# Attention: K padded per head by GpSimd, Q dense for four heads, batch loop written out

## What is computed

```python
def _L1_attn_ref(x, w_in, b_in, w_out, b_out):
    B, S, E, H = (2, 256, 128, 16)
    ...
    qkv = x @ w_in.T + b_in
    q, k, v = jnp.split(qkv, 3, axis=-1)
    ...
    scores = jnp.einsum('bhqd,bhkd->bhqk', q * scale, k)
    ...
    attn = jax.nn.softmax(scores, axis=-1)
    out = jnp.einsum('bhqk,bhkd->bhqd', attn, v)
```

## Time and profile before

| | |
|---|---|
| median of three runs | 2952.7 us |
| span of the profiled execution | 3037.0 us |
| attention phase in it | about 1973 to 2772 us |
| TensorE busy, matmuls, of the span | 84% |
| VectorE busy | 75% |
| ScalarE busy | 59% |
| GpSimd busy | 45% |

### The profile page before, as it was taken

One profiled execution on the slowest core, in us unless ns is written; L12 is line 12 of the kernel. 1 busy time (PEld: TensorE's weight loads), 2 busy tenths in 40 slices (PEclk: granted clock), 3 DMA queues, 4 the chain that ended last, 5 costly groups with the idle time before them and its releaser, 6 DMA issues. The chain is left out here.

```text
span 3037.0 us, 38397 instructions
## 1 busy us (share of the span) xinstructions
PE 2549.4 (84%) x11128; PEld 1669.2 (55%) x11128; DVE 2285.1 (75%) x3877; ACT 1790.3 (59%) x3099; POOL 1373.7 (45%) x1486
## 2 busy tenths in 40 slices
PE   6888477888888888868887689969988889887999
PEld 5766233343344344227676568746555556554887
DVE  6887478989999999998786544478777777774444
ACT  3566465657556656524666445547777667665555
POOL 2365488888988988961563630021121121111000
PEclk9999688999999999998998789979999999998999
DMA  2246222222222222221345200020000000001000
GB/s 69 55 130 123 79 68 67 75 69 72 70 74 74 77 73 74 77 71 39 75 130 96 73 21 1 0 95 1 1 1 1 2 1 1 1 1 39 7 8 14
DMA packets 99804, 152.38 MB, mean 50 GB/s; under 512 B 12940, under 2 KB 50572, under 8 KB 99028
## 3 DMA queue, kind: packets, MB, share of 16 engines
q1 hardware_dynamic: 82052, 98.41, 10.6%
q0 software_dynamic: 17040, 51.07, 6.8%
q10 hardware_dynamic: 512, 0.53, 0.1%
HBM read 131.08 MB, written 18.87 MB: 49 GB/s over the span
## 5 line engine op out<-in xcount | busy, mean ns | idle before, releaser
L1750 POOL TENSOR_TENSOR a_hc<-a_H,a_cb 128x512 f32<-128x512 f32 x512 | 620.0, 1233 | 134.3 <-DVE a_H L1614 127.3
L1406 PE MATMUL a_Y<-a_hc,ident 128*128 128x512 f32 x1024 | 535.3, 633 | 57.0 <-POOL a_hc L1750 48.6
L2216 DVE TENSOR_REDUCE a_mx<-a_W 128x1 f32<-128x512 f32 (+3 forms) x768 | 397.2, 550 | 153.3 <-PE a_W L2005 99.6
L2116 ACT ACTIVATE a_pt<-a_W 128x512 f32<-128x512 f32 (+3 forms) x768 | 353.5, 493 | 224.1 <-PE a_W L2018 220.7
L1532 ACT ACTIVATE a_dA<-a_dt,a_aneg 128x512 f32<-128x512 f32 x512 | 342.6, 714 | 193.8 <-POOL a_dt L1769 103.2
L1406 PEld LDWEIGHTS a_Y<-a_hc,ident 128*128 128x128 f32 x1024 | 183.0, 196 | 307.6 <-POOL a_hc L1750 212.7
L1638 DVE TENSOR_TENSOR a_BX<-a_u,a_BX 128x1024 f32<-128x1024 f32 x256 | 308.6, 1211 | 44.0 <-PE a_BX L1340 22.3
L1614 DVE TENSOR_TENSOR_SCAN a_H<-a_dA,a_H,a_BX 128x512 f32<-128x512 f32 x256 | 312.5, 1264 | 2.5 <-ACT a_dA L1532 2.5
L2018 PE MATMUL a_W<-a_Q,a_K 128*128 128x512 f32 (+3 forms) x768 | 302.3, 399 | 4.1 <-ACT a_pt L2116 2.0
L1614 DVE TENSOR_TENSOR_SCAN a_H<-a_dA,a_BX 128x512 f32<-128x512 f32 x256 | 296.7, 1202 | 1.1 <-POOL a_hc L1750 1.0
L2002 PE MATMUL a_W<-a_K,a_Q 128*128 128x512 f32 (+3 forms) x768 | 273.9, 363 | 20.4 <-DVE a_K L2283 9.9
(11 more groups left out here) (327 smaller groups left out, 5628.4 us busy)
## 6 DMA issues: line engine op xcount, KB each, us to landing
a_cb<-a_crow SPq DMA_DIRECT2D x256, 256.0 KB, 3.1
m_orows<-m_yt SPq DMA_DIRECT2D x46, 256.0 KB
a_Q<-attention_zeros POOLq DMA_DIRECT2D x3, 2048.0 KB, 13.3
t_wst<-ternary_w SPq DMA_DIRECT2D x22, 256.0 KB, 2.7
m_xrows<-m_pool SPq DMA_DIRECT2D x16, 256.0 KB, 2.3
m_xg<-m_xrows,m_gidx POOLq DMA_INDIRECT x184
out<-x SPq DMA_DIRECT2D x8, 256.0 KB, 2.3
m_wg<-moe_ws SPq DMA_DIRECT2D x2, 516.0 KB, 4.5
```

The lines of the kernel that those rows point to most:

```text
L1406: pe.matmul(Y[:, h, :], ident[:], hc[:, g % HCRING, :], start=False, stop=v == NS - 1).then_inc(s_y, 1)
L1750: pool.tensor_tensor(hc[:, G % HCRING, :], H[:, s, span], cb[:, v % RING, :], ALU.mult).then_inc(s_hc, 1)
L2116: act.activation(pt[:, u % PR, 0:BLK - r * P], W[:, 3 + u % 3, 0:BLK - r * P], ACT.Exp).then_inc(s_exp, 1)
L2216: dve.tensor_reduce(dst, W[:, s % 3, 0:min(BLK, (t + 1) * P - c * BLK)], AX, ALU.max)\
```

## The change

K is padded in place of Q. K now has a copy per head and Q one dense tile per group. VectorE's combination of K lands in `stk`; GpSimd multiplies `stk` by a column of `heads` (one on the head's 32 rows, zero elsewhere) into each head's copy (`keys`): 128x512, four per chunk, eight per slot. Q's combination lands in Q directly. ScalarE's copies are gone, as are the zeroing of Q and the three transfers; a small load of `heads` is new. K is projected first (uses 0 and 2), Q afterwards (4 and 5). The maxima are added to Q in one addition of 128 rows. In GpSimd's queue two multiplications stand behind the mask of step 2, two behind that of step 3, and four behind the split of the maxima that follows. In the pre slot sixteen stand ahead of the first split. The loop over sequences 1 and 2 is a Python loop, all waits are on constants.

```diff
-            uses.update({0: ("Q", rel, n, 0), 2: ("Q", rel, n, 1), 4: ("K", rel, n, 0), 5: ("K", rel, n, 1),
+            uses.update({0: ("K", rel, n, 0), 2: ("K", rel, n, 1), 4: ("Q", rel, n, 0), 5: ("Q", rel, n, 1),
                          6: ("V", rel, n // 2, n % 2)})
...
-        with eng.Fori(1, NBATCH - 1) as i:
+        for i in range(1, NBATCH - 1):
...
-        Q, K = sb("Q", [P, GROUPS * GH, SEQ], F32R), sb("K", [P, GROUPS, SEQ], F32R)
+        Q, K = sb("Q", [P, GROUPS, SEQ], F32R), sb("K", [P, GROUPS * GH, SEQ], F32R)
...
-        ZEROS = tuple((Q[:, n:n + GH, :].rearrange("p h c -> p (h c)"), w["zeros"].bitcast(F32R))
-                      for n in range(GH, GROUPS * GH, GH))
...
-                    pe.matmul(W[:, 3 + u % 3, 0:BLK - r * P], K[:, g, tile(kt)],
-                              Q[:, g * GH + j, c * BLK + r * P:(c + 1) * BLK],
+                    pe.matmul(W[:, 3 + u % 3, 0:BLK - r * P], K[:, g * GH + j, tile(kt)],
+                              Q[:, g, c * BLK + r * P:(c + 1) * BLK],
...
-                                    pe.wait_ge(s_q, 2 * G + 4)
+                                    pe.wait_ge(s_k, 2 * G + 4)
...
-                def queries(i, use, j):
...
-                    last = act.activation(Q[head(j), n * GH + j, chunk(c)], stk[head(j), c, :], ACT.Copy)
...
-                    if kind == "max" and j < 2:
-                        for jj in (2 * j, 2 * j + 1):
-                            q = Q[head(jj), n * GH + jj, chunk(c)]
-                            ins = dve.tensor_tensor(q, q.bitcast(F32), M[head(jj), :], ALU.add)
-                        if j == 1:
-                            last = ins
+                    if kind == "max" and j == 0:
+                        q = Q[:, n, chunk(c)]
+                        last = dve.tensor_tensor(q, q.bitcast(F32), M[:], ALU.add)
...
-                for dst, src in ZEROS:
-                    pool.dma_start(dst, src).then_inc(s_zero, 16)
                 pool.wait_ge(s_xn, 1)
-                pool.memset(Q[:, 0:GH, :].bitcast(F32), 0.0).then_inc(s_cst, 1)
...
+                def keys(G, n, c, js):
+
+                    if js[0] == 0:
+                        pool.wait_ge(s_ld, 16 * len(LOADS))
+                        pool.wait_ge(s_st, 4 * G + c + 1)
+                    for j in js:
+                        last = pool.tensor_scalar(K[:, n * GH + j, chunk(c)], stk[:, c, :].bitcast(F32),
+                                                  heads[:, j:j + 1], 1.0, ALU.mult, ALU.mult)
+                    if js[-1] == GH - 1:
+                        last.then_inc(s_k, 1)
+
                 def slot(stage, i, g):
                     G = i * GROUPS + g
+                    n = (g + 2) % GROUPS
+                    ahead = stage not in ("last", "tail") or (stage == "last" and g + 2 < GROUPS)
+                    if stage == "pre":
+                        keys(0, 0, 0, range(GH))
+                        keys(0, 0, 1, range(GH))
+                        keys(1, 1, 0, range(GH))
+                        keys(1, 1, 1, range(GH))
                     if has_exp(stage):
                         split_max(stage, i, g, G, g, 1)
                         for v in DIAG[:TPB]:
                             mask_step(i, g, v)
+                            if ahead and v >= 2:
+                                keys(G + 2, n, 0, range(2 * (v - 2), 2 * (v - 1)))
                     if has_max(stage, g):
                         split_max(stage, i, g, G + 1, (g + 1) % GROUPS, 0)
                     if has_exp(stage):
+                        if ahead:
+                            keys(G + 2, n, 1, range(GH))
                         for v in DIAG[TPB:]:
                             mask_step(i, g, v)
```

More of the change, by code:

```diff
@@ L1895, in has_max, with all_slots @@
         return stage != "tail" and not (stage == "last" and g + 1 == GROUPS)
-    def all_slots(slot, eng):
+    def all_slots(slot):
         slot("pre", 0, -1)
@@ L1920, in attention @@
         wo, bo = sb("wo", [P, P]), sb("bo", [P, P])
-        mask = sb("mask", [P, P])
+        mask, heads = sb("mask", [P, P]), sb("heads", [P, GH])
         idr, mneg = sb("idr", [P, P], F32R), sb("mneg", [P, P], F32R)
-        stk = sb("stk", [P, 2, BLK])
+        stk = sb("stk", [P, 2, BLK], F32R)
         mhalf, zero = sb("mhalf", [P, TILES]), sb("zero", [P, TPB, GH])
@@ L1948, in attention @@
         s_ld, s_cst, s_wh, s_pre = sem("ld"), sem("cst"), sem("wh"), sem("pre")
-        s_zero, s_bsc = sem("zeros"), sem("bsc")
+        s_bsc = sem("bsc")
         s_mv, s_ve, s_rstd = sem("mv"), sem("ve"), sem("rstd")
@@ L1961, in attention @@
                  (scale[:], w["scale"]), (low[:], w["low"]), (wo[:], w["w_out"]), (bo[:], w["b_out"]),
-                 (mask[:], w["mask"]))
-        ZEROS = tuple((Q[:, n:n + GH, :].rearrange("p h c -> p (h c)"), w["zeros"].bitcast(F32R))
-                      for n in range(GH, GROUPS * GH, GH))
+                 (mask[:], w["mask"]), (heads[:], w["heads"]))
         def early(v):
@@ L2001, in max_unit @@
                     out = W[:, s % 3, 0:cols]
-                    mm = pe.matmul(out, Q[:, g * GH + j, tile(t)], K[:, g, c * BLK:c * BLK + cols],
+                    mm = pe.matmul(out, Q[:, g, tile(t)], K[:, g * GH + j, c * BLK:c * BLK + cols],
                                    start=True, stop=not diag)
@@ L2040, in m_use @@
                     if early(v):
-                        if kind == "Q" and c == 0:
+                        if kind == "K" and c == 0:
                             pe.wait_ge(s_Md, through("D", stage, i, g, v - 1))
@@ L2097, in slot @@
                             m_use(stage, i, g, v, uses[v])
-                all_slots(slot, pe)
+                all_slots(slot)
             @block.scalar
@@ L2145, in m_read @@
                             act.activation(oT[:, c, :], M[:], ACT.Copy).then_inc(s_Ma, 1)
-                def queries(i, use, j):
-                    if isinstance(i, int) and i == 0 and use[2] == 1 and j == 0:
-                        act.wait_ge(s_zero, 16 * len(ZEROS))
-                    kind, rel, n, c = use
-                    G = (i + rel) * GROUPS + n
-                    if j == 0:
-                        act.wait_ge(s_st, 4 * G + c + 1)
-                    last = act.activation(Q[head(j), n * GH + j, chunk(c)], stk[head(j), c, :], ACT.Copy)
-                    if j == GH - 1:
-                        last.then_inc(s_q, 1)
                 def slot(stage, i, g):
@@ L2173, in slot @@
                                 m_read(stage, i, before[1], before[2], before[0], j)
-                            copied = copies(stage, g, v)
-                            if copied:
-                                queries(i, copied, j)
-                all_slots(slot, act)
+                all_slots(slot)
             @block.vector
@@ L2275, in stack @@
                     G = (i + rel) * GROUPS + n
-                    m, k = (c, n) if kind == "Q" else (2 + c, GROUPS + n)
+                    m, k = (c, GROUPS + n) if kind == "K" else (2 + c, n)
                     dve.wait_ge(s_Ma, through("A", stage, i, g, v))
-                    if kind == "Q":
-                        wait(dve, s_q, 2 * (G - 1) + c + 1)
+                    if kind == "K":
+                        wait(dve, s_k, 2 * (G - 1) + c + 1)
                         out = stk[:, c, :]
                     else:
-                        out = K[:, n, chunk(c)]
+                        out = Q[:, n, chunk(c)]
                     dve.scalar_tensor_tensor(out, qh[:, m % 2, :].bitcast(F32), low[:, k:k + 1],
@@ L2313, in _ @@
                 chain = [None]
-                all_slots(slot, dve)
+                all_slots(slot)
             @block.gpsimd
@@ L2371, in slot @@
                     if has_exp(stage):
+                        if ahead:
+                            keys(G + 2, n, 1, range(GH))
                         for v in DIAG[TPB:]:
                             mask_step(i, g, v)
-                all_slots(slot, pool)
+                all_slots(slot)
         ph.clear()
@@ L2525, in attention_layout @@
         "w_out": g("w_out").T, "b_out": np.broadcast_to(g("b_out"), (P, P)),
-        "mask": np.triu(np.full((P, P), -1e30, np.float32), 1), "zeros": np.zeros((P, 4096), np.float32),
+        "mask": np.triu(np.full((P, P), -1e30, np.float32), 1), "heads": np.repeat(np.eye(GH, dtype=np.float32), ROWS, 0),
     }
```

17 lines of the change are left out of this document (6 added, 11 removed).

## The result

The changed kernel takes **2885.3 us** (median of 4 runs, 2883.6 to 2886.2) against 2955.3 for the kernel before beside it (2952.7 to 2961.3): ratio 0.976, 95% interval 0.975 to 0.978, 70 us off. The forecast was 54 us off and 2899 us, with a range of 2880 to 2935; the time lies in the range, 14 us under the forecast.

What follows compares the result with a forecast made beforehand. TensorE's own work plus 4.4 us of waits per slot bound the attention phase. Terms -25.6 - 20.5 - 6.4 - 1.9 - 6 + 4 + 3 - 2 = -55.4 us, scaled to -54: 2899 us, range 2880 to 2935.

Steps and rivals of the forecast that it cites:

- The copies: Attention steps 9 and 10: without ScalarE's Q copies the value products wait 1.83 us less in each of 14 slots, 25.6 us off.
- Step 1's wait: Value products of step 1 wait for a mask slowed (1.14 us for 0.64) by VectorE's combination; claimed to stay, 0 gain.
- if step 1's waits shrink too: Best end of the range: 2880 us in place of 2886, should the mask waits at step 1 shrink.
- The additions: TensorE's waits for VectorE adding the maxima to Q, mostly at step 2: all 20.5 us go with one 128-row addition.
- the reductions: TensorE's waits for VectorE's reductions, which queue behind the additions of the maxima to Q: all 6.4 us go.
- T: Time of one GpSimd 128x512 multiplication, eight per slot: taken as 0.64 us from the mask's select, 1.28 kept for the range.
- the start: First score product of the attention phase, behind eight multiplications: claimed unmoved at 0.64 us each, 5.1 us later at 1.28.
- Mask 2 and contention: Charges: step 2's mask late by 0.3 us in 14 slots, 4 us; VectorE's combinations meeting GpSimd's multiplications at SBUF, 3 us.
- The pre slot: Slot without exps at the phase's start: VectorE loses three additions of 0.68 us, 2 us off, between 0 and 2.
- The blocked combination: VectorE combinations and GpSimd multiplications excluding each other for whole instructions: 36 us if all four were blocked; not expected so often.
- Loop and clock: Batch loop's one jump written out, 1.9 us off; less TensorE time at the lower clock, 6 us off, between 0 and 12.
- The scale of 0.97: Profiled span 3037.0 us against the runs' median 2952.7, so the 55.4 us gain was scaled to 54.

## Why the prediction was right, point by point

- **The copies** (25.6): right. The steps gave 1.93 us per slot in place of 1.83, and putting copies back took 27 us at these two steps.
- **Step 1's wait** (0): the step that failed. The prediction saw that the combination stays at its place in VectorE's order and took from that that it stays first in time. It was first by 0.10 us, and in the changed kernel the exps that the mask waits for end sooner by as much. The wait went in all 13 slots that had it, 0.61 us each or 8 in all. It listed this only as an end of the range, "if step 1's waits shrink too". With the copies put back those exps were late again; how copies at steps 9 and 10 reach step 1 of the next slot was not found.
- **The additions** (20.5) and the reductions (6.4): right in the sum. In slots 0 to 13 step 2 gave 20.2 us and step 8 gave 7.8, some of it clock, against 26.9. An undisturbed slot had 1.24 us at step 2 for the 1.1. The reductions were mis-sized: their waits went, as forecast, but in eight slots the value products of step 8 then wait for the mask, and of 0.53 us only 0.23 was won. The price of an addition by its columns held: 0.675 us on 128 rows. But the additions are worth this only while the combination is first (31.8 us). With the mask first they are worth over 60 us.
- **The multiplications**: T = 0.67 for the 0.64 taken from the mask's row, and the start moved by 0.5 us for the 0 forecast. The Trainium skill ("GPSIMD Engine Reference", section 3.1) gives 769 ns for a loop over 512 elements; back to back these rows show 671.
- **Mask 2 and contention** (+4, +3): mis-sized, no cost of either shows. Seven us too dear. Combinations were held up, to 1.2 us at steps 1 and 3 of all 14 slots, but by the selects and not by the multiplications, and TensorE waited for none of them.
- **The pre slot** (2): right. From the first score product to the first value product it took 35.9 us before and 33.6 after.
- **The blocked combination.** The Trainium skill ("SBUF — State Buffer", section Who interferes with whom) has the two exclude each other for the whole instruction. That would be 0.63 + 0.74 = 1.37 us for a combination that starts with the select, and 0.74 - 0.10 + 0.64 = 1.28 us for a select that starts 0.10 behind the combination; the rows have 1.17 and 1.14. So here it is most of the instruction, one engine pays all of it, and that is the later one except in near ties, which VectorE loses.
- **Loop and clock** (1.9 + 6): in the slots and behind them the lower level took 31 us before and 14 after, which at half speed is at most 8.5; with the jump it comes near the forecast. Alone, the unrolled kernel before gained 4.1 us by the medians and nothing in its trace, and the changed kernel lost 10 to 13 with the loop, so the two can't be told apart as terms.
- **The scale of 0.97**: wrong in kind, small in size (1.4 us). The 84 us lay outside the phase and do not stretch it.

The sum of 55.4 with 8 for step 1, and without the two charges of 7, is 70.4; the phase lost 69.1. That they agree so well is in part luck, as two traces of equal kernels differ by 3. By steps the traces give: ahead of slot 0 1.8 us; in slots 0 to 13 64.9, of which 8.0 at step 1, 28.0 at steps 2 and 8, 23.9 at steps 9 and 10, and 5.0 at the others, mostly at step 11 where the jump was; behind them 2.3.

## What to carry to other kernels

An operation's place in an engine's order does not say whether it is first at SBUF; its start does, and where two start within some 0.1 us of each other, both outcomes belong in the sum, with the engine that pays in each. Waits of parts don't add: price each edit on the schedule that the others leave, and ask whether two short waits join into one of 2 us. What a cheap engine carries ahead of the work that everybody waits for (a 0.14 us operation ahead of a mask) can be worth its time at step after step (here at five of twelve), even where no row shows a wait.

## What was not expected of the hardware

- One 128x1 addition on GpSimd (0.19 us) per slot made one kernel 11.1 us slower and another, the same but for the additions to Q, faster: by 24.5 us in the phase of single traces, by some 18 in the medians.
- Of a select and a combination that meet at SBUF, VectorE's combination is held up even when it starts 0.06 us ahead; at 0.09 us ahead it is GpSimd's select.
- The clock: waits of 2.08 us at one step per slot came with 105.6 us at the lower level, waits of 0.74 and 1.04 in place of them with 58.0; waits of 2.06 for the mask with 88.7. Kernels that wait little still have 38 to 45 us of it (51 in one), 31 to 34 of them in the first 70 us of the phase.
- Two-input GpSimd multiplications with one input broadcast along the row: 1.0 us for 512 columns; the two-input addition of the earlier trace rows took 1.27.
- Executions that run this phase in the same time reach it at 1888 us on one chip and at 1958 to 1974 on others. (Before, on the faster chip: 2955.3 less 1888.4 ahead, 265.0 behind and 2.1 around the span is 799.8 us for the phase, and 799.5 in the trace of the other.)
